# Both heads of a pair side by side in the attention, and a 1024-token feed-forward pass at the end

## The reference

```python
q, k, v = (proj(Wq), proj(Wk), proj(Wv))      # of layernorm(x); 16 heads of 64
scores = jnp.einsum('bhqd,bhkd->bhqk', q, k) * SCALE
w = jax.nn.sigmoid(scores)
w = w / (w.sum(axis=-1, keepdims=True) + EPS)
out = jnp.einsum('bhqk,bhkd->bhqd', w, v)     # then @ Wo.T
x = x + layernorm(attention)
h = silu((y @ w1.T) * w1_s) * ((y @ w2.T) * w2_s)   # y = layernorm(x), 1024 -> 4096
h = gelu((h @ h1.T) * h1_s)                         # 4096 -> 4096
h = gelu((h @ h2.T) * h2_s)                         # 4096 -> 4096
x = x + layernorm((h @ w3.T) * w3_s)                # 4096 -> 1024
```

## Time and profile before

| | |
|---|---|
| median of 3 runs | 10431.25 us (10384.3 to 10434.22) |
| the profiled execution | 10400.06 us, its slowest core's span 10398.5 us |
| spans of the 8 cores | 10283.9 to 10398.5 us |
| granted TensorE clock, mean of each core | 0.705 to 0.722 of 2.4 GHz |
| TensorE matmul busy | 7944.4 us (76%) |
| ScalarE busy | 3095.9 us (30%) |
| VectorE busy | 910.4 us (9%) |
| the 16 DMA engines, mean | 64 GB/s |

### The profile page before, as it was taken

How to read it: one execution, slowest core, us unless ns; L and a number is a source line. 1 busy time by engine, 2 the same in 40 slices (tenths; PEclk the granted TensorE clock), 3 DMA queues, 4 the chain that set the end, 5 groups by cost and what they waited for, 6 DMA issues and landing times.

```text
span 10398.5 us, 75322 instructions; the slowest of 8 cores (10283.9 to 10398.5 us)
## 1 busy us (share of the span) xinstructions
PE 7944.4 (76%) x22936; PEld 2445.6 (24%) x22936; DVE 910.4 (9%) x740; ACT 3095.9 (30%) x3645; POOL 291.8 (3%) x589
## 2 busy tenths in 40 slices
PE   5554556999999985788875788879899865885786
PEld 1221221222222221232321223221111112332332
DVE  3132130000000021100000100010000031001001
ACT  0000002444444423343324334425445410001000
POOL 0000000000000000000000000000000001000000
PEclk7776776555555556788876888965555569998998
DMA  3847745011111112444432444420000025664665
GB/s 105 25 77 76 34 84 38 33 33 33 33 33 33 33 32 65 69 83 86 81 70 47 81 86 82 91 62 23 31 31 22 31 59 82 123 128 79 104 126 104
DMA packets 320768, 663.09 MB, mean 64 GB/s; under 512 B 153760, under 2 KB 219296, under 8 KB 270624
## 3 DMA queue, kind: packets, MB, share of 16 engines
q0 software_dynamic: 79056, 379.62, 20.9%
q1 hardware_dynamic: 241360, 278.65, 15.3%
HBM read 987.04 MB, written 50.72 MB: 100 GB/s over the span
## 4 chain that ended last, share of the span: by engine, by line
PE 63%; DMA 21%; ACT 6%; issue 5%; DVE 4%; SPq 0%; ACTq 0%; DVEq 0%; POOLq 0%
PE psO L599 17%; PE psS L563 16%; PE psG L901 16%; DMA V_sc<-vvo 6%; DMA wfb<-h 5%; PE psF L856 5%; ACT wtil L574 3%; DMA wfb<-w 3%; PE psP L353 3%; DMA kbuf<-K_sc 2%; PE psW L940 2%; DMA xs<-xT 2%; ACT L574 2%; DMA y1f<-y_sc 1%; PE ps_sum L306 1%
## 5 line engine op out<-in xcount | busy, mean ns | idle before, releaser
L574 ACT ACTIVATE wtil<-psS 128x512 bf16<-128x512 f32 (+1 forms) x2752 | 2190.3, 805 | 3020.8 <-PE psS L563 3004.5
L599 PE MATMUL psO<-wtil,vbuf 128*65 128x512 bf16 x4096 | 2121.0, 586 | 607.8 <-ACT wtil L574 496.5
L563 PE MATMUL psS<-qbuf,kbuf 64*128 64x512 bf16 x4096 | 2044.1, 568 | 280.3 <-DMA kbuf<-K_sc 280.3
L901 PE MATMUL psG<-fb,wfb 128*128 128x512 bf16 x8192 | 2054.1, 412 | 185.8 <-DMA wfb<-h 157.7
L901 PEld LDWEIGHTS psG<-fb,wfb 128*128 128x128 bf16 x8192 | 830.6, 104 | 1351.4 <-issue 681.8
L599 PEld LDWEIGHTS psO<-wtil,vbuf 128*65 128x65 bf16 x4096 | 497.2, 138 | 2092.3 <-issue 2089.3
L563 PEld LDWEIGHTS psS<-qbuf,kbuf 64*128 64x128 bf16 x4096 | 387.2, 108 | 1846.0 <-issue 1837.9
L404 PE MATMUL psV<-wvb,lnb 128*128 128x512 bf16 x1024 | 333.6, 501 | 324.7 <-DVE vvo L416 313.9
L619 DVE COPY rs_row<-psO 1x512 f32<-1x512 f32 x64 | 43.8, 685 | 5344.5 <-PE psO L599 5344.5
L856 PE MATMUL psF<-ln2tB,wfb 128*128 128x512 bf16 x1024 | 262.9, 405 | 257.5 <-DMA wfb<-w 233.8
L300 ACT ACTIVATE sq<-xs 128x2048 bf16<-128x2048 f32 x32 | 61.1, 1909 | 1209.2 <-DMA xs<-xT 1209.2
(11 more groups left out here) (104 smaller groups left out, 2220.1 us busy)
## 6 DMA issues: line engine op xcount, KB each, us to landing
wfb<-h POOLq DMA_DIRECT2D x256, 1024.0 KB, 8.5
vbuf<-V_sc SPq DMA_DIRECT2D x512, 130.0 KB, 2.1
xs<-xT SPq DMA_DIRECT2D x64, 1024.0 KB, 4.9
kbuf<-K_sc SPq DMA_DIRECT2D x32, 2048.0 KB, 7.9
wfb<-w POOLq DMA_DIRECT2D x256, 256.0 KB, 3.8
wfb<-w POOLq DMA_DIRECT2D x32, 1024.0 KB, 8.5
V_sc<-vvo SPq DMA_DIRECT2D x64, 260.0 KB
K_sc<-kvo SPq DMA_DIRECT2D x32, 512.0 KB, 2.6
```

The lines of the kernel that those rows point to most:

```text
L563: inst = e.matmul(psS[p][:, j * QM:(j + 1) * QM], kbuf[kp][b:b + 64, (k0 + j) * 128:(k0 + j + 1) * 128], self.qbuf[b:b + 64, hp_ * T + q0: ...
L574: self.emit("act", lambda e, p=spar, n=nk, psS=psS: e.activation(wtil[p][:, 0:n * QM], psS[p][:, 0:n * QM], AF.Sigmoid, scale=ATT_SCALE), ...
L599: inst = e.matmul(psO[op][:, :], vbuf[vp][:, a_ * (DH + 1): a_ * (DH + 1) + DH + 1], wtil[spar][:, j * QM:(j + 1) * QM], start=(k == 0), s ...
L901: inst = e.matmul(psF[p][:, tt * NT:(tt + 1) * NT], wfb[b][:, ic * 128:(ic + 1) * 128], s[:, ic * th + tt * NT: ic * th + (tt + 1) * NT], ...
```

## The change

In the attention, the two heads of a pair are no longer done one after the other but together: a tile is `kct` chunks of both heads. The scores of the two heads alternate matmul by matmul, head 0 into `psS[0]` and head 1 into `psS[1]`. So `psS` no longer alternates from tile to tile: the scores of a tile wait until both sigmoids of the tile before have read it. `wtil` and the V buffers go from 2 to 4. In the interleaved stage `kct` goes from 1 to 2. In stage B one pass of 1024 tokens takes the place of two passes of 512. In `gen_phase3` the squares and column sums of the w3 part move behind the whole of it, into a loop of their own (so that PSUM holds it), and the generator gives one step more per w3 block. The warm-up matmuls at the start of each attention stage go from 32 to 16.

```diff
         if qms_b:
             with ExitStack() as pctx:
-                psS, psO = p1_psums(pctx, 1, nkb=1)
-                g_mid = self.gen_phase1(qms_b, 1, psS, psO)
+                psS, psO = p1_psums(pctx, 2, nkb=1)
+                g_mid = self.gen_phase1(qms_b, 2, psS, psO)
...
-            for t0f in range(TW, T, 512):
-                for _ in self.gen_phase3(t0f, 512, ln2tB, TW, TW):
+            for t0f in range(TW, T, 1024):
+                for _ in self.gen_phase3(t0f, min(1024, T - t0f), ln2tB, TW, TW):
...
-                            for _ in range(32):
+                            for _ in range(16):
                                 inst = e.matmul(psS[1][:, 0:NT], self.warmsrc[:, 0:128],
...
-                    for hh in range(2):
-                        h = 2 * hp + hh
-                        hb = hh * 64
-                        opar = h % 2
-                        pending_pv = None
...
+                    pending_pv = None
+                    v_lds = {}
+                    for ti, (kc0, nk) in enumerate(tiles):
+                        for kc in range(kc0, kc0 + nk):
+                            if kc % 8 == 0:
+                                kb = kc // 8
+                                for hh in range(2):
+                                    vslot = hh * 2 + kb % 2
...
+                        def mk_sc(e, kp=kpar, k0=kc0, n=nk, hp_=hp, q0=q0):
+                            for j in range(n):
+                                for hh in range(2):
+                                    b = hh * 64
                                     inst = e.matmul(
-                                        psS[p][:, j * QM:(j + 1) * QM],
+                                        psS[hh][:, j * QM:(j + 1) * QM],
                                         kbuf[kp][b:b + 64, (k0 + j) * 128:(k0 + j + 1) * 128],
...
+                        self.emit("pe", mk_sc,
+                                  waits=[(f"ld_k{kpar}", k_ld)] + psS_free[0] + psS_free[1],
+                                  incs=[("pe", 1)])
+                        sc_done = self.c("pe")
+                        sig_done = [0, 0]
+                        tp_ = ti % 2
+                        for hh in range(2):
+                            w = hh * 2 + tp_
+                            self.emit("act", lambda e, w=w, hh=hh, n=nk: e.activation(
+                                wtil[w][:, 0:n * QM], psS[hh][:, 0:n * QM],
                                 AF.Sigmoid, scale=ATT_SCALE),
...
+                            sig_done[hh] = self.c("act")
+                            psS_free[hh] = [("act", sig_done[hh])]
+
+                        if pending_pv is not None:
+                            pending_pv()
...
+                        def mk_pv_emit(k0=kc0, n=nk, sig=tuple(sig_done), tp_=tp_,
+                                       vw=(tuple(vwaits[0]), tuple(vwaits[1]))):
+                            for hh in range(2):
+                                w = hh * 2 + tp_
+                                def mk_pv(e, hh=hh, w=w):
...
+                        pending_pv = mk_pv_emit
+                        yield
+                    pending_pv()
+                    pending_pv = None
+                    pv_all = self.c("pe")
+                    for hh in range(2):
+                        h = 2 * hp + hh
+                        self.emit("dve", lambda e, hh=hh: e.tensor_copy(
+                            rs_row[hh][:], psO[hh][64:65, :]),
...
+                            yield
+
+                    with ExitStack() as p3ctx:
+                        ps3s = p3ctx.enter_context(nc.psum_tensor(self.u("ps3s"), [1, th], F32))
+                        ps3q = p3ctx.enter_context(nc.psum_tensor(self.u("ps3q"), [1, th], F32))
+                        f_done = self.c("dve")
+                        sq_free = [[], []]
+                        for oc in range(NCD):
+                            par = oc % 2
                             self.emit("act", lambda e, o=oc, p=par, fbf=fbf, sq3=sq3: e.activation(
                                 sq3[p][:], fbf[:, o * th:(o + 1) * th], AF.Square),
-                                waits=[("dve", fv)] + sq_free[par], incs=[("act", 1)])
+                                waits=[("dve", f_done)] + sq_free[par], incs=[("act", 1)])
```

More of the change, by code:

```diff
@@ L173, in p1_psums @@
             self.wtil = [pctx.enter_context(nc.sbuf_tensor(self.u(f"wtil{i}"), [128, kct * 512], BF16))
-                         for i in range(2)]
-            self.wtil_free = [self.guard(), self.guard()]
+                         for i in range(4)]
+            self.wtil_free = [self.guard() for _ in range(4)]
             self.kbuf = [pctx.enter_context(nc.sbuf_tensor(self.u(f"kbuf{i}"), [128, S], BF16))
@@ L490, in open_p1 @@
         self.rs_free = [[], []]
-        self.vbuf_free = [[], []]
+        self.vbuf_free = [[], [], [], []]
     def gen_phase1(self, qms, kct, psS, psO):
@@ L568, in mk_sc @@
                                         start=True, stop=True)
[L569 to L575, removed]
+                            return inst
@@ L576, in gen_phase1 @@
                                 AF.Sigmoid, scale=ATT_SCALE),
-                                waits=[("pe", sc_done)] + wtil_free[spar],
+                                waits=[("pe", sc_done)] + wtil_free[w],
                                 incs=[("act", 1)])
[L579 to L585, removed]
+                            sig_done[hh] = self.c("act")
@@ L597, in mk_pv @@
                                         a_ = k % 8
-                                        vp = (k // 8) % 2
+                                        vslot = hh * 2 + (k // 8) % 2
                                         inst = e.matmul(
-                                            psO[op][:, :],
-                                            vbuf[vp][:, a_ * (DH + 1): a_ * (DH + 1) + DH + 1],
-                                            wtil[spar][:, j * QM:(j + 1) * QM],
+                                            psO[hh][:, :],
+                                            vbuf[vslot][:, a_ * (DH + 1): a_ * (DH + 1) + DH + 1],
+                                            wtil[w][:, j * QM:(j + 1) * QM],
@@ L622, in gen_phase1 @@
-                        rsd = self.c("dve")
[L623 to L629, removed]
+                                        vbuf_free[hh * 2 + (kc // 8) % 2] = [("pe", self.c("pe"))]
@@ new lines, in gen_phase1 @@
+                        pending_pv = mk_pv_emit
[3 more added lines that the diff above has]
+                    pv_all = self.c("pe")
+                    for hh in range(2):
+                        h = 2 * hp + hh
+                        self.emit("dve", lambda e, hh=hh: e.tensor_copy(
+                            rs_row[hh][:], psO[hh][64:65, :]),
+                            waits=[("pe", pv_all)] + rs_free[hh], incs=[("dve", 1)])
+                        rsd = self.c("dve")
+                        self.emit("sy", lambda e, hh=hh, h=h, q=q0: e.dma_start(
+                            self.RS_sc[h:h + 1, q:q + QM], rs_row[hh][:]),
+                            waits=[("dve", rsd)], incs=[(f"st_v{hh}", 16)])
+                        rs_free[hh] = [(f"st_v{hh}", self.c(f"st_v{hh}"))]
+                        self.emit("dve", lambda e, hh=hh, c=hp, q=q0: e.tensor_copy(
+                            self.obuf[hh * 64:hh * 64 + 64, c * T + q: c * T + q + QM],
+                            psO[hh][0:64, :]),
@@ L972, in mk_stats @@
                                 return inst
-                            self.emit("pe", mk_stats, waits=[("act", actv), ("dve", fv)],
+                            gw = self.guard() if oc == 0 else []
+                            self.emit("pe", mk_stats, waits=[("act", actv)] + gw,
                                       incs=[("pe", 1)])
```

46 lines of the change are left out of this document (19 added, 27 removed).

## The result

The changed kernel takes 8251.93 us (median of 9 runs, 8204.54 to 8527.57) against 10431.29 us (median of 10 runs, 10344.58 to 10515.49). The ratio is 0.7905, 95% interval 0.7873 to 0.7937. Forecast were 8650 us and a range from 8400 to 9460: the direction was right, the gain is 2180 us instead of 1780, and the time lies under the range.

What follows compares the result with a forecast made beforehand. It took TensorE to bound stage A, a lone attention tail to be the interleaved stage's largest loss, and weight loads to bound stage B. Gains 427 + 1075 + 260 + 10 (warm-up) = 1772 gave 8650 us, range 8400 to 9460.

Steps and rivals of the forecast that it cites:

- Bounds of the kernel before: Stage A by TensorE, the interleaved stage by its 1436 us attention tail, stage B by weight loads.
- Part 1: Stage A attention: a serial loop of 4.15 us per tile, mostly at 2.4 GHz; 1626 us, a gain of 427.
- three slots for six scores: Attention tiles in stage A: both heads' score matmuls run at the same time; six slots if one after the other.
- Part 2: Interleaved stage: attention ends after 264 rounds, the rest is feed-forward alone; 3309 us in all, a gain of 1075.
- the 8% added for waits and clock: Interleaved h layers: added to 17.2 us per block of two rounds, giving 18.6 us, K loads counted apart.
- K loads 16 x 8 = 128: Interleaved stage: 128 us for K loads, part of it lying under feed-forward matmuls.
- Part 3: Stage B in one pass: h layers turn from load-bound to TensorE-bound; gain 240 at clock 0.81, 455 at 1.00, 260 taken.
- The slowest core decides, so I take 260: Stage B: 260 us taken as gain, between 240 at a clock of 0.81 and 455 at 1.00.
- better than forecast: Stage B at a clock of 1.00 and stage A tiles at 4.04 us: under 8400 us, chance 4%.
- The clock staying at 1.2 GHz: Attention: scores overlap but waits for sigmoids hold the clock down; about 9450 us, chance 12%.
- no overlap: Attention: the two heads' matmuls don't overlap; gains about 30 + 740 + 270, about 9400 us, chance 17%.
- the slower serial loop: Attention: scores don't overlap, clock 1.2 GHz, weight loads exposed; stage A cycle 6.5 us, about 10850 us, chance 5%.

Runs made afterwards that it cites:

- same_rows: The changed kernel with both heads' score matmuls reading partitions 0 to 63, order, waits and sizes unchanged; ratio 0.8594, fastest run 8882.57 us.
- grouped: The changed kernel with a tile's scores issued head by head, all of head 0 then all of head 1, same buffers and waits; fastest run 8276.29 us, no interval.

## Why the prediction was off

The three stages gained 2127 us on core 4, the forecast had 1772, so 355 us too little. Another 76 us lie between the forecast and core 4's 8203 us because the forecast started from the slowest core (10398 us before) and core 4 took 10322. The last sum is also rounded down: 8628 + 31 is 8659, not 8650.

**Bounds of the kernel before**: right on all three stages; each was relieved where it said.

**Part 1, stage A.** The largest choice, three slots for six scores, was right, and so was the serial loop and the rise of the clock; of the reason given for the rise, same_rows fits the part on the scores (with head 1's on head 0's rows the clock is 0.74 instead of 0.91), and the V products in sixes were not tested by themselves. The size was off by 88 us (515 for 427). The cycle was taken as 4.15 us; it is 3.91. Of the difference, 0.11 us is the term "from a sigmoid's end to the matmul that waits for it ... I take 0.25 us" (0.14 measured), and 0.11 us the share of time at 1.2 GHz that was added to 4.04. 0.24 x 336 = 81 us. The stop between pairs, taken as 10.7 us, was 11.4 us (170.3 over 15).

**Part 2, interleaved stage.** 1165 instead of 1075 us. 2 x 64 table loads, 264 rounds and the vanished tail came as forecast, and the rest alone took 534 + 122 us for 546 + 149. The h layers took the 1190 us of the forecast, but by two errors that cancel: the 1190 measured contain 83 us of waits for K, which the forecast counted apart. Without them a block took 17.3 us, next to the 17.2 reckoned; the 8% added for waits and clock, 88 us over 64 blocks, was too much. In the same way w1 and w2, 552 us for 572, contain 33 us of K. The term "K loads 16 x 8 = 128" was itself too small: the waits for K came to 168 us. Against the forecast, the w3 and output part took 335 us, not 285, 41 of them for K.

**Part 3, stage B: the step that failed.** "The slowest core decides, so I take 260" chose the clock of 0.81 for the h layers. On core 4 they ran at 1.00, 889 us instead of 1088, and stage B gave 447 us, next to the 455 that the text had as the other end. This one choice is 187 of the 355 us. Both values stood in the earlier trace rows had 0.97 for core 3 over the 546 us of these very layers; one core's row of 50 us in phase 0 was made the rule for a long stretch elsewhere. The Trainium skill, "TensorE: Matmul & The Clock Gate", Part 1, has a limit of 13/16 for a whole die once three of its cores run dense matmuls. The trace does not agree for this kernel: from 7300 to 7900 us all eight cores were in dense matmuls, the four cores of core 4's die had 1.00, and on the other die cores 0 and 1 had 0.84 while cores 2 and 3 had 1.00. What sets 0.84 or 1.00 stays open. The weights of these layers are -1, 0 or 1 and those of phase 0, where the 0.81 was read, are not; no run changed the values.

**Part 4, the range.** The three sizes erred the same way, 88 + 90 + 187, and "better than forecast" had 4%. The range's lower end lay 250 us under the forecast although one term alone, stage B's clock, was 215 us wide. Ends that are known to be that far apart belong in the range in full.

**Rivals.** The clock staying at 1.2 GHz, no overlap, and the slower serial loop didn't occur. The second can be priced now: with matmuls on one row group (same_rows) the kernel takes 8883 us, not 9400. Stage A gained 192 us there where the rival had 30 (its clock was 0.74), the interleaved stage 827 where it had 740, and stage B 447 where it had 270.

## What to carry to other kernels

Two heads of 64 side by side on the two halves of TensorE's rows cost the time of one (six scores in 0.82 us, against 1.45 on one half), so pairing was worth more here than buffering the heads one after the other. But put the pair in one PSUM tile and keep two or three such tiles, or scores and sigmoid become a serial loop (3205 against 2712 us here; in stage A 1366 against 1008, K loaded ahead in both). When a change makes TensorE the bound of a stage, keep the whole span between the clocks that the rows show (0.81 and 1.00 here) in the range. Look at what stands ahead of a prefetch in its queue: the K loads were held by a store of 2 KB, and moving their issue forward gave 176 us.

## What the hardware showed that was not expected

- TensorE overlaps matmuls of different row groups that are three places apart in its list (grouped: from six scores to the products 0.76 us at 2.4 GHz and 1.40 us at 1.2 GHz, the former as when they alternate).
- A stretch in which TensorE is busy less can have the higher clock: stage A had 0.52 at 91% busy before, 0.91 at 52% after, and 0.74 at 70% in same_rows. From after to same_rows only the rows of head 1's scores differ, and with them the time that the scores take; between before and same_rows several things differ, and no run takes them apart.
- In one execution the same dense stretch of stage B ran at 1.00 on core 4 and at 0.84 on core 0 (889 and 1043 us), and core 3, on core 0's die, had 1.00 in it.
